# Self-attention scores for 32x32 diagonal blocks only, one softmax per step, and an unsplit float32 value product

## What is computed

```python
qkv = jnp.einsum('sbh,ph->sbp', tokens, weight_qkv)      # S=16, B=128, H=1024, P=6144
# 8 groups: 4 query heads, one key head, one value head, each of 128
scores = jnp.einsum('bhsd,bhtd->bhst', q, k) * scale     # 16x16 per sequence and head
scores = jnp.where(causal, scores, jnp.finfo(scores.dtype).min)
attn = jax.nn.softmax(scores, axis=-1)
out = jnp.einsum('bhst,bhtd->bhsd', attn, v)
return jnp.einsum('sbe,he->sbh', out, weight_proj)
```

## Time and profile before

| what | value |
|---|---|
| median of three runs | 3785.24 us (3785.0 to 3787.38) |
| span of the profiled execution | 3789.7 us |
| self-attention phase in it | from 11.3 us (first load) to 2215.1 us (last sum) |
| PE busy | 3586.1 us, 95% of the span |
| DVE, ACT, POOL busy | 1870.1, 1315.5 and 1281.4 us |
| one step of the middle of the phase | 67.2 us |

### The profile page before, as it was taken

One profiled execution on the slowest core, in us unless ns is written; L12 is line 12 of the kernel. 1 busy time (PEld: TensorE's weight loads), 2 busy tenths in 40 slices (PEclk: granted clock), 3 DMA queues, 4 the chain that ended last, 5 costly groups with the idle time before them and its releaser, 6 DMA issues. The chain is left out here.

```text
span 3789.7 us, 51735 instructions
## 1 busy us (share of the span) xinstructions
PE 3586.1 (95%) x18740; PEld 2841.5 (75%) x18740; DVE 1870.1 (49%) x2810; ACT 1315.5 (35%) x1903; POOL 1281.4 (34%) x562
## 2 busy tenths in 40 slices
PE   6999999999999999999999869999999999997999
PEld 5888877888887888888878747777777777773487
DVE  3444364343453544445444435665665665652354
ACT  3233243333332323333233224454454544440100
POOL 4333343343433434334343333343343444320000
PEclk9999999999999999999999979999999999998899
DMA  4222233232323322323222144455546455443032
GB/s 172 78 100 94 84 132 123 89 105 83 113 98 123 111 84 99 115 79 139 72 88 72 34 146 125 128 162 159 141 145 173 132 155 168 128 109 156 21 129 83
DMA packets 137257, 431.21 MB, mean 114 GB/s; under 512 B 24112, under 2 KB 24112, under 8 KB 137144
## 3 DMA queue, kind: packets, MB, share of 16 engines
q1 hardware_dynamic: 131384, 408.58, 34.6%
q10 hardware_dynamic: 5760, 20.97, 1.4%
HBM read 316.21 MB, written 37.75 MB: 93 GB/s over the span
## 5 line engine op out<-in xcount | busy, mean ns | idle before, releaser
L439 POOL TENSOR_TENSOR sa_wl<-sa_wraw,sa_wh 128x1024 fp32r<-128x1024 f32 x192 | 472.5, 2468 | 1130.6 <-ACT sa_wh L601 1130.6
L51 PE MATMUL sa_u<-sa_ln_xh,sa_wh 128*128 128x512 f32 x1536 | 614.6, 400 | 3.9 <-DVE sa_ln_xl L248 3.9
L52 PE MATMUL sa_u<-sa_ln_xl,sa_wh 128*128 128x512 f32 x1536 | 599.0, 390 | 5.4 <-issue 5.4
L53 PE MATMUL sa_u<-sa_ln_xh,sa_wl 128*128 128x512 f32 x1536 | 600.9, 391 | 0.0
L768 DVE TENSOR_TENSOR sa_acc<-sa_pr,sa_acc 128x512 f32<-128x512 f32 x256 | 177.1, 692 | 827.4 <-PE sa_pr L53 827.3
L450 POOL TENSOR_TENSOR sa_pl<-sa_praw,sa_ph 128x1024 fp32r<-128x1024 f32 x128 | 336.0, 2646 | 239.3 <-ACT sa_ph L653 239.3
L51 PE MATMUL sa_pr<-sa_ph,sa_oh 128*128 128x512 f32 x1024 | 413.2, 404 | 2.5 <-DVE sa_ol L761 2.4
L52 PE MATMUL sa_pr<-sa_pl,sa_oh 128*128 128x512 f32 x1024 | 406.2, 397 | 0.0
L53 PE MATMUL sa_pr<-sa_ph,sa_ol 128*128 128x512 f32 x1024 | 405.3, 396 | 0.0
L53 PEld LDWEIGHTS sa_u<-sa_ln_xh,sa_wl 128*128 128x128 f32 x1536 | 288.9, 188 | 68.7 <-issue 5.8
L51 PEld LDWEIGHTS sa_u<-sa_ln_xh,sa_wh 128*128 128x128 f32 x1536 | 289.6, 189 | 59.7 <-issue 2.7
(11 more groups left out here) (195 smaller groups left out, 6750.7 us busy)
## 6 DMA issues: line engine op xcount, KB each, us to landing
sa_wraw<-in_wqkv SPq DMA_DIRECT2D x192, 512.0 KB, 3.5
sa_praw<-in_wproj SPq DMA_DIRECT2D x128, 512.0 KB, 3.5
ca_wraw<-w_folded SPq DMA_DIRECT2D x96, 512.0 KB, 3.3
ca_kstack<-ca_kmh SPq DMA_DIRECT2D x256, 128.0 KB, 2.4
ca_wraw<-in_wo SPq DMA_DIRECT2D x33, 512.0 KB, 4.2
ca_kstack<-ca_kml SPq DMA_DIRECT2D x128, 128.0 KB, 2.4
ca_qstack<-ca_qh SPq DMA_DIRECT2D x256, 64.0 KB, 2.6
sa_nat<-in_w_nat SPq DMA_DIRECT2D x24, 512.0 KB, 4.4
```

What stands on the lines that cost most here:

```text
L51: nc.tensor.matmul(out, ah, bh, start=(first and i == 0), stop=False)
L52: nc.tensor.matmul(out, ah, bl, start=False, stop=False)
L53: ins = nc.tensor.matmul(out, al, bh, start=False, stop=(last and i == len(parts) - 1))
L439: nc.gpsimd.tensor_tensor(wl[:, u % 3], wraw[:, u % 3], f32(wh[:, u % 3]), ALU.subtract).then_inc(w_split, 1)
```

## The change

- The scores are computed for the four 32x32 blocks on the diagonal of a tile, with keys on the partitions: the key columns of a block are the stationary operand (128x32), the queries of all four heads for the same 32 tokens the moving one (128x128), and the result lies on 32 partitions. All four tiles of a step share one PSUM bank, 16 products in a row.
- One softmax for the whole step, 128 partitions x 16 blocks x 32. Since it needs the keys along the row, DVE transposes the masked scores in 32x32 blocks (`nc.vector.transpose`), and after the softmax transposes them back, in four instructions of 32 partitions each, into `diag`, a buffer that is zero outside the blocks. POOL clears it once.
- `turn_probs`, and the splits of the probabilities and of the values, go. The value product is one float32 matmul per tile, v by `diag`, 128x128 by 128x512, into one of two PSUM banks; `oh` and `ol` have two buffers.
- The order of the work in a step changes on every engine, as the diff shows. ACT starts with `exps()`, ahead of `out_weights([0, 1])`.
- The mask is built transposed, with four small copies at the start.

```diff
+            nc.gpsimd.memset(diag[:], 0.0).then_inc(diag_zeroed, 1)
...
+                    pe.wait_ge(s_masked, m + 1)
+                    for t in range(TILES):
+                        for q in range(QUADS):
+                            rows = slice(q * QW, (q + 1) * QW)
+                            cols = slice(t * P + q * QW, t * P + (q + 1) * QW)
+                            ins = nc.tensor.matmul(s_ps[rows, t * P:(t + 1) * P], kT[:, mp, cols], qT[:, mp, :, cols],
+                                                   start=True, stop=True)
...
-                    three_passes(nc, o_ps[:], [(vh[:, mp, t], vl[:, mp, t], probsTh[:], probsTl[:])]
-                                 ).then_inc(o_done, 1)
+                    heads = slice(t * QPG, (t + 1) * QPG)
+                    nc.tensor.matmul(o_ps[t % 2][:], v[:, mp, t], diag[:, heads].rearrange("p h q n -> p (h q n)"),
+                                     start=True, stop=True).then_inc(o_done, 1)
...
-                scores(0)
+                scores()
                 unit(0)
-                turn_probs(0)
-                scores(1)
                 unit(1)
-                mix_values(0)
-                turn_probs(1)
-                scores(2)
                 unit(2)
                 turn_v()
-                project(0)
-                mix_values(1)
-                turn_probs(2)
-                scores(3)
+                mix_values(0)
                 unit(3)
                 fold_half(0)
-                project(1)
-                mix_values(2)
-                turn_probs(3)
+                mix_values(1)
+                project(0)
                 unit(4)
                 fold_half(1)
-                project(2)
+                mix_values(2)
+                project(1)
                 mix_values(3)
                 unit(5)
                 if s.norm:
...
                     turn_groups(s.b + 1, range(4))
+                project(2)
                 project(3)
...
+                exps()
                 out_weights([0, 1])
-                exps(0)
                 copy_unit(0)
-                copy_probs(0)
                 out_weights([2, 3])
...
+                    nc.vector.transpose(probs[:].rearrange("p k n -> p (k n)"),
+                                        masked[:].rearrange("p k n -> p (k n)")).then_inc(s_turned, 1)
...
+                    dve.wait_ge(probs_ready, i)
+                    dve.wait_ge(diag_zeroed, 1)
+                    dve.wait_ge(o_done, m * TILES + 1)
+                    for q in range(QUADS):
+                        rows = slice(q * QW, (q + 1) * QW)
+                        nc.vector.transpose(diag[rows, :, q], probs[rows]).then_inc(diag_ready, 1)
...
-                softmax(0)
-                low_probs(0)
-                softmax(1)
+                softmax()
                 low_o(0)
-                low_probs(1)
-                softmax(2)
-                low_v()
-                add_projected(0)
                 next_moments(0)
                 low_o(1)
-                low_probs(2)
-                softmax(3)
                 next_moments(1)
+                add_projected(0)
+                next_moments(2)
+                next_moments(3)
+                low_o(2)
                 add_projected(1)
-                next_moments(2)
-                low_o(2)
-                low_probs(3)
-                next_moments(3)
-                add_projected(2)
+                low_o(3)
```

More of the change, by code:

```diff
@@ L30 @@
 SELF_SCALE = 1.0 / HD ** 0.5
+QW = 32
+QUADS = P // QW
 CH = D // P
@@ L129, in _ @@
                                     ALU.add).then_inc(mix_steps, 1)
+            for q in range(QUADS):
+                rows = slice(q * QW, (q + 1) * QW)
+                nc.vector.tensor_copy(causal_t[rows], causal[rows, rows])
             dve.wait_ge(small_loaded, 48)
@@ L321, in self_attention_phase @@
         vT = sb("sa_vT", [P, BT])
[L322 to L331, removed]
+        v = sb("sa_v", [P, 2, TILES, HD])
+        BLK = TILES * QPG
+        masked = sb("sa_masked", [P, BLK, QW])
+        probs = sb("sa_probs", [P, BLK, QW])
+        diag = sb("sa_diag", [P, BLK, QUADS, QW])
+        top = sb("sa_top", [P, BLK])
+        total = sb("sa_total", [P, BLK])
+        inv = sb("sa_inv", [P, BLK])
+        oh = sb("sa_oh", [P, 2, QPG * P], F32R)
+        ol = sb("sa_ol", [P, 2, QPG * P], F32R)
         nat = sb("sa_nat", [P, D])
@@ L336, in self_attention_phase @@
         pr_ps = [bank(f"sa_pr{i}") for i in range(2)]
-        s_ps, t_ps, o_ps, v_ps = bank("sa_s"), bank("sa_t"), bank("sa_o"), bank("sa_vt")
-        turn_ps = [s_ps, t_ps, o_ps, v_ps]
+        s_ps, v_ps = bank("sa_s"), bank("sa_vt")
+        o_ps = [bank(f"sa_o{i}") for i in range(2)]
+        turn_ps = [s_ps, o_ps[0], o_ps[1], v_ps]
         wraw_loaded = [sem(f"sa_wraw_loaded{i}") for i in range(3)]
@@ L464, in _ @@
             pe.sem_inc(folded, 2)
+            pe.sem_inc(o_done, 1)
             def turn_groups(b, rs):
@@ L510, in fold_half, with scores @@
                     ins.then_inc(folded, 1)
-                def scores(t):
+                def scores():
                     if not s.attn:
                         return
[L515 to L522, removed]
-                    ins.then_inc(s_done, 1)
[L525 to L532, removed]
+                    pe.wait_ge(u_copied, n * U + 2)
+                    if s.cross:
+                        pe.wait_ge(ln.lo_done, s.b * ln.GROUPS + 5)
+                    pe.wait_ge(s_masked, m + 1)
[5 more added lines that the diff above has]
+                                                   start=True, stop=True)
+                    ins.then_inc(s_done, 1)
                 def mix_values(t):
@@ L653, in out_weights, with exps @@
                         nc.scalar.activation(ph[:, h], praw[:, h], ACT.Copy).then_inc(p_hi, 1)
-                def exps(t):
+                def exps():
                     if not s.attn:
                         return
-                    act.wait_ge(s_shifted, m * TILES + (t + 1))
+                    act.wait_ge(s_shifted, m + 1)
                     nc.scalar.activation(probs[:], probs[:], ACT.Exp, scale=SELF_SCALE).then_inc(exp_done, 1)
-                def copy_probs(t):
-                    if not s.attn:
-                        return
-                    act.wait_ge(probs_turned, m * TILES + (t + 1))
-                    nc.scalar.activation(probsTh[:], t_ps[:], ACT.Copy).then_inc(probsT_hi, 1)
                 def high_o(t):
@@ L696, in step @@
                 store_fold()
+                if s.norm:
+                    ln.deviations(act, s.b + 1)
+                high_o(2)
                 high_o(3)
```

89 lines of the change are left out of this document (35 added, 54 removed).

## The result

The changed kernel takes 3616.5 us (3613.6 to 3619.0, four runs), the kernel before, timed beside it, 3786.3 us (3785.0 to 3788.9): a ratio of 0.9547, 95% interval 0.9535 to 0.9560. That is 170 us less, where 144 were forecast. That end, 3616 us, stood 169 us under the kernel before as timed then, so by the gain the result is a hair outside.

What follows compares the result with a forecast made beforehand. PE's own instruction list was taken as the bound; 31 steps at 4.84 less 0.40 give 137.6, the last step 6.6, 0.5 back: 143.7 off the 3789.7 span is 3646.0, a median of 3642 us; range 3616 to 3688.

Steps and rivals of the forecast that it cites:

- The bound: In the self-attention step PE's own list sets the time; it gets 4.84 us shorter, to 62.4.
- The scores: At the step's start, 32 small float32 instructions run beside each other, busy 1.06 us; 1.30 us added to PE.
- Rival 2: The small scores don't run beside each other: 2.2 us more each step, 3710 us; chance 0.07.
- The value product: One float32 product per tile takes 0.86 us on PE; four cost 3.62 a step, against 2.80 for the three passes.
- The 2 x 0.09 on top: Lag of the next matmul behind float32 work, 0.09 us, charged to two of a step's four value products.
- The new wait: In each step PE would wait 0.4 us ahead of unit(3) for POOL's weight, a tie of 19.0 against 18.8.
- The transposes: DVE's first softmax transpose takes 0.69 us; the four into diag, about 0.72 each, up to 1.65, stay hidden.
- Rivals 1 and 3: Slow transposes or a worse meeting with POOL, 3682, chance 0.14; DVE holding POOL off, 3778 to 3887, chance 0.05.
- What isn't touched costs the same: Unstated in the sum: matmuls the change leaves alone, as in project and units, keep their cost, a difference of nothing.
- The last step: The 32nd step, attention alone, starts project(0) at 16.3 behind POOL's four pl and takes 43.1 us, 6.6 less.
- The range: Total time from 3616 (no wait, cheaper scores, long waits gone) to 3688 (slow transposes or worse meeting, scores at 1.5).
- the long waits of the earlier trace: Two long PE waits, gone with the burst of loads spread out: 8 us less, counted in the low end only.

Runs made afterwards that it cites:

- The loops exchanged: The changed kernel with the two loops of the score products exchanged, so four in a row write the same 32 partitions: 3658.5 us, ratio 0.9654.
- the two with halves: The changed kernel with each value product as two float32 products on halves of the rows: 3611.8 us; with 64 unused bytes ahead of sa_oh too: 3608.4 us.

## Why the prediction was right and where it was wrong

**Where it failed.** The path was right: PE's own list, which got shorter by what the trace of before priced. The size was not: 4.44 us a step were forecast, and 5.48 came on average, 5.60 in an ordinary step. Two terms of the sum carry most of it. All matmuls that the change doesn't touch were taken to cost what they cost before, a difference of nothing for which no reason was given; measured are 0.46 us a step for `project` alone, 14 us in all. And 0.40 us a step, 12 us in all, were put down for a wait ahead of `unit(3)` that isn't there.

**The bound: right.** PE's own list sets the step, before and after. DVE's 12 us less a step bought only what the transposes had waited for it.

**The scores: right.** 1.08 us for 32 instructions as the cross-attention's rows had it, bracket 1.21 for 1.30. The moving operand in four pieces costs nothing. The loops exchanged show what the order is worth. Rival 2 didn't come.

**The value product: right but for the exit.** 0.86 from start to start was right to the hundredth. The 2 x 0.09 on top were counted twice: 0.18 a step, 6 us. (Three of the four, not two, stand behind other float32 work, `turn_v` and `fold_half`. And the 12 matmuls by 0.23 that go are 2.76 and not 2.80, 0.04 the other way.)

**The new wait: wrong, and it was the close call.** The chain (mask, transpose, softmax, `ph`, four `pl`, `wl`) was right in each link, and delaying it by 1.46 us brought the wait at the place named. PE's side was right too: 18.8 was summed, and the value product ahead of `unit(3)` starts at 17.90 and holds PE for 0.86. What failed is the price of POOL's list. `wl` was due 19.0 us behind the scores and is ready at 18.0. An undisturbed `pl` or `wl` takes 2.36 to 2.38 from start to start, and the meeting costs POOL 0.46 once: 12.3. The 13.3 of the prediction had the meeting in each of the five (2.6, from a pair) and 0.3 for it besides. 0.1 came back at POOL's start. So it wasn't a tie: the slack is 0.6. The 0.4 that I took are 12 us in all.

**The transposes: right.** 0.71 us and 0.70 each beside a busy POOL. Rivals 1 and 3 rested on a transpose being held up or holding POOL off, and it does neither. The other half of rival 1, a meeting that costs POOL 0.7 and not 0.3, came in part (0.46), in a list that was 1.0 shorter than summed.

**What isn't touched costs the same: wrong.** This term isn't in the sum at all. The two kernels differ in the distance of `sa_oh` from `sa_ph`, 96 against 192 modulo 256, and it is worth 0.0048 us a matmul, 96 matmuls a step: 0.46 us, 14 us in all. The runs bound it from both kernels: 14 us when 32 bytes take the good distance from the changed kernel, 16 us when 96 bytes give it to the kernel before. Of the 170 us, some 155 are left for what the change meant to do; the changed kernel at a distance of 224, about as slow as 96, takes 3630 us, inside the range. The 0.10 of the units is open: their distance is 0 in both kernels, and it is 0.2271 or 0.2272 in the kernels derived from the changed one, at any distance of `project`, and 0.2275 in the two with halves. For this part less work beside PE (theory B) isn't excluded.

**The last step: right in kind.** 40.5 for 43.1. POOL's four `pl` are done 15.4 us behind the scores, forecast 16.3. And the slow clock is paid by two value products ahead of a wait for `pl` that PE has anyway, as its timeline shows (scores at 1996.97):

```profile
2008.63 3.75 PE L544 MATMUL sa_o<-sa_diag,sa_v 128*128 128x512 f32 x4 [10.58 <-issue]
2012.46 0.74 PE L53 MATMUL sa_pr<-sa_ph,sa_oh 128*128 128x512 f32 x1
```

The granted clock is 0.50 from 2008.63 to 2012.46, the lower of the two levels (1.2 GHz), after PE had stood for 10.58 us. The two products have their place in 3.83, where they take 1.72 at full clock, and `pl` is ready only at 2012.40. From 2012.46 to the end of the last sum at 2037.44 it is 25.0, where 26.8 were summed.

**The range.** It was built from the wait, the scores and the loads. A term of plus or minus 15 us for the placement of buffers was missing, and the low end, 3616, was reached with it. The 8 us that I had put there for the long waits of the earlier trace rows didn't come: those waits grew from 5.4 to 9.5 us.

## What to carry to other kernels

When an edit adds, drops or resizes a buffer, compare the start-to-start spacing of matmuls that the edit doesn't touch; if it moved, the edit changed a placement, and unused bytes ahead of a buffer show it and often mend it. Here the best distance between the starts of stationary and moving operand was a multiple of 256 bytes. Small products are cheap when neighbours write different groups of 32 partitions and many stand in one row; two pairs alone gave back at their edges and between them nearly all that they won. Where two engines meet at shared ports, both can pay: here the one that came 0.01 us later lost 2.3 us and the other 0.46 in its next instruction. And a duration taken as the mean of a few instructions may hold such a meeting already, so read them one by one.

## What was not expected of the hardware

- Matmuls of 512 fp32r columns start 0.227 to 0.234 us apart by the distance of their two operands in SBUF. 64 bytes ahead of one buffer made this kernel 31 us slower, 96 bytes made the kernel before 16 us faster, and the same shift of all buffers did nothing.
- Products with 32 stationary columns start 0.026 apart when neighbours write different groups of 32 partitions, and 0.071 when they write the same.
- DVE's transpose of 128x512 float32 numbers in 32x32 blocks lasts 0.71 us, as long as an addition of that size, and four of 32x512 last 0.70 each beside a busy POOL.
- A multiplication of two SBUF tensors that starts 0.01 us behind POOL's subtraction lasts 2.95 in place of 0.69, and POOL's next instruction 2.86 in place of 2.40, in every step, while a transpose beside the same POOL isn't held up (0.70).
